# The first microseconds of a gated low-rank kernel: when GpSimd and VectorE subtract, and in which order TensorE takes tile 2

## The reference

```python
base = jnp.einsum('btd,od->bto', x, W)
logits = jnp.einsum('btd,ed->bte', x, Wr)
logits = logits + one_hot(expert_targets, E) * LANG_BIAS          # 5.0
topw, topi = jax.lax.top_k(logits, 2)
weights = jax.nn.softmax(topw, axis=-1)
gates = jnp.sum(one_hot(topi, E) * weights[..., None], axis=-2)
h = jnp.einsum('btd,erd->bter', x, A)                              # E = 8, R = 16
lora_out = jnp.einsum('bter,bte,eor->bto', h, gates, B)
return x + base + 2.0 * lora_out
```

## Time and profile before

| | us |
|---|---|
| median of three runs | 80.66 |
| lowest and highest | 80.62, 80.95 |
| the profiled execution | 80.91 |
| its span, first to last instruction | 79.1 |

### The profile page before, as it was taken

One profiled execution on the slowest core, in us unless ns is written; L12 is line 12 of the kernel. 1 busy time (PEld: TensorE's weight loads), 2 busy tenths in 40 slices (PEclk: granted clock), 3 DMA queues, 4 the chain that ended last, 5 costly groups with the idle time before them and its releaser, 6 DMA issues.

```text
span 79.1 us, 1627 instructions
## 1 busy us (share of the span) xinstructions
PE 75.2 (95%) x505; PEld 71.2 (90%) x505; DVE 49.4 (62%) x219; ACT 22.2 (28%) x56; POOL 24.0 (30%) x26
## 2 busy tenths in 40 slices
PE   6999999799999999999999999999999999999960
PEld 2379997699999999999999999999999999999950
DVE  0099498878692828475483928284664829787670
ACT  4334951514231414050322314140503113111200
POOL 4035697062350241406060503315060605000000
PEclk9999999999999999999999999999999999999999
DMA  1999994489379199998920000270000063032024
GB/s 11 292 321 355 401 420 202 50 364 391 38 273 413 75 227 440 418 298 353 413 109 3 0 0 0 99 298 0 0 0 0 0 264 134 0 133 103 34 102 164
DMA packets 3748, 14.23 MB, mean 180 GB/s; under 512 B 416, under 2 KB 1056, under 8 KB 3488
## 3 DMA queue, kind: packets, MB, share of 16 engines
q1 hardware_dynamic: 3600, 13.98, 48.4%
q10 hardware_dynamic: 144, 0.20, 0.8%
HBM read 9.99 MB, written 4.19 MB: 179 GB/s over the span
## 4 chain that ended last, share of the span: by engine, by line
PE 78%; DMA 8%; DVE 6%; SPq 2%; ACT 1%; issue 1%; DVEq 0%
PE heads_ps L412 36%; PE base_ps L412 25%; DMA first_sb<-in_first 8%; PE heads_ps L444 5%; PE base_ps L444 5%; DVE w_lo L345 3%; PE base_ps L448 2%; PE heads_ps L448 2%; PE ghT_ps L435 2%; SPq L167 1%; ACT w_hi L228 1%; SPq L165 1%; DVE top_atf L297 1%; DVE out_sb L331 1%; ACT x_hi L225 1%
## 5 line engine op out<-in xcount | busy, mean ns | idle before, releaser
L205 POOL TENSOR_TENSOR x_lo<-xT_sb,x_hi 128x512 fp32r<-128x512 f32 x14 | 18.2, 1303 | 37.4 <-ACT x_hi L235 37.4
L412 PE MATMUL heads_ps<-w_hi,x_hi 128*128 128x392 f32 x64 | 22.7, 366 | 0.0
L412 PE MATMUL heads_ps<-w_hi,x_lo 128*128 128x392 f32 x64 | 21.4, 342 | 0.0
L412 PE MATMUL heads_ps<-w_lo,x_hi 128*128 128x392 f32 x64 | 21.1, 339 | 0.0
L412 PE MATMUL base_ps<-w_hi,x_hi 128*128 128x256 f32 x64 | 17.7, 287 | 0.0
L412 PE MATMUL base_ps<-w_hi,x_lo 128*128 128x256 f32 x64 | 17.6, 281 | 0.0
L412 PE MATMUL base_ps<-w_lo,x_hi 128*128 128x256 f32 x64 | 17.5, 282 | 0.0
L281 DVE TENSOR_TENSOR ghT_lo<-ghT_ps,ghT_hi 128x128 fp32r<-128x128 f32 x15 | 4.3, 290 | 15.2 <-ACT ghT_hi L239 15.2
L412 PEld LDWEIGHTS heads_ps<-w_hi,x_hi 128*128 128x128 f32 x64 | 12.0, 192 | 1.1 <-ACT x_hi L225 0.6
L239 ACT ACTIVATE ghT_hi<-ghT_ps 128x128 fp32r<-128x128 f32 x15 | 4.1, 277 | 30.8 <-PE ghT_ps L435 30.8
L412 PEld LDWEIGHTS base_ps<-w_lo,x_hi 128*128 128x128 f32 x64 | 12.1, 189 | 0.3 <-DVE w_lo L345 0.3
(11 more groups left out here) (43 smaller groups left out, 93.4 us busy)
## 6 DMA issues: line engine op xcount, KB each, us to landing
x_sb<-in_x SPq DMA_DIRECT2D x4, 768.0 KB, 5.6
out<-out_sb SPq DMA_DIRECT2D x4, 768.0 KB, 4.2
xT_sb<-in_xT SPq DMA_DIRECT2D x3, 768.0 KB, 4.3
first_sb<-in_first SPq DMA_DIRECT2D x3, 454.0 KB, 5.5
xT_sb<-in_xT SPq DMA_DIRECT2D x1, 1024.0 KB, 6.4
x_sb<-in_x SPq DMA_DIRECT2D x1, 1024.0 KB, 11.1
out<-out_sb SPq DMA_DIRECT2D x3, 256.0 KB, 2.0
xT_sb<-in_xT SPq DMA_DIRECT2D x1, 256.0 KB, 6.4
```

The source lines that it names most:

```text
L205: nc.gpsimd.tensor_tensor(x_lo[:, s, :], xT_sb[:, t - len(FIRST), :], x_hi[:, s, :].bitcast(FP32), ALU.subtract).then_inc(x_lo_made, 1)
L412: return nc.tensor.matmul(dst, xs[:, s, chunks[k]], ws[:, k, cols], start=(k == 0 and n == 0), stop=(k == KC - 1 and n == last_n))
```

## The change

Four things change, all of them before tile 3:

1. VectorE also rounds the heads columns of w_hi in chunk 2, which ScalarE did together with the base columns. TensorE's waits follow that.
2. GpSimd waits until all eight low-weight subtractions are done before x_lo of tile 2.
3. GpSimd waits for gh of tile 0 before b_lo.
4. TensorE takes the heads products of tile 2 in another order: first the eight that need only x_hi, then, one ahead of the transpose of tile 0 and three behind it, those with x_lo.

```diff
+            pool.wait_ge(w_lo_made, 2 * KC)
             x_lower(2, 2)
             pool.wait_ge(b_hi_made, 1)
+            pool.wait_ge(gh_made, 1)
             nc.gpsimd.tensor_tensor(b_lo[:, :], b_sb[:, :], b_hi[:, :].bitcast(FP32),
                                     ALU.subtract).then_inc(b_lo_made, 1)
...
-                w_upper(k, base_cols if k == 1 else all_cols)
+                w_upper(k, base_cols if k < KC - 1 else all_cols)
...
-            dve.wait_ge(chunk_landed[0], 16)
-            heads_upper(1)
-            dve.wait_ge(wh_hi_made, 2)
-            w_lower(1, heads_cols)
-            dve.wait_ge(w_hi_made, 2)
-            w_lower(1, base_cols)
-            for k in range(2, KC):
+            for k in range(1, KC - 1):
+                dve.wait_ge(chunk_landed[k - 1], 16)
+                heads_upper(k)
+                dve.wait_ge(wh_hi_made, k + 1)
+                w_lower(k, heads_cols)
                 dve.wait_ge(w_hi_made, k + 1)
-                w_lower(k, heads_cols)
                 w_lower(k, base_cols)
+            dve.wait_ge(w_hi_made, KC)
+            w_lower(KC - 1, heads_cols)
+            w_lower(KC - 1, base_cols)
...
-                if k == 1:
-                    pe.wait_ge(wh_hi_made, 2)
+                if k < KC - 1:
+                    pe.wait_ge(wh_hi_made, k + 1)
                 else:
-                    pe.wait_ge(w_hi_made, k + 1)
+                    pe.wait_ge(w_hi_made, KC)
                 for t in FIRST:
                     heads_product(t, k, 0)
-                if k == 1:
-                    pe.wait_ge(w_hi_made, 2)
+                pe.wait_ge(w_hi_made, k + 1)
...
-            tile_ready(2)
-            heads(2, (0, 1))
+            pe.wait_ge(x_hi_made, 1)
+            for k in range(KC):
+                for n in range(2):
+                    heads_product(2, k, n)
+            pe.wait_ge(x_lo_made, 1)
+            heads_product(2, 0, 2)
             pe.wait_ge(ident_made, 1)
             transpose(0, 0)
-            heads(2, (2, 3)).then_inc(heads_done, 1)
+            for k in range(1, KC):
+                last = heads_product(2, k, 2)
+            last.then_inc(heads_done, 1)
```

## The result

The changed kernel takes 82.21 us in the median of four runs (82.06 to 82.96), against 80.81 for the kernel before on the same chip. The ratio is 1.0161, with a 95% interval from 1.0117 to 1.0205. It is slower, as forecast, but by 1.3 to 1.4 us where 0.83 was forecast, and outside the range. Its profiled execution took 82.06 us with a span of 80.3.

The account below looks back on a forecast made before the run. TensorE, busy 75.2 of 79.1 us, was taken as the bound. Early gains put it 0.86 us ahead, but held VectorE instructions moved tile 1's transpose from 16.77 to 17.60: 80.66 + 0.83, given as 81.5 us, range 80.5 to 82.0.

Parts of the forecast that it names:

- The tile 0 part of the sum: TensorE up to the first lora product: transpose of tile 0 at 14.17 instead of 14.50, 0.86 us ahead by lora.
- the hold of the cast of tile 1: VectorE's top-index cast (top_atf) starts at 14.75 inside GpSimd's b_lo and ends at 15.45 instead of 14.92, 0.53 us late.
- x_lo of tile 3 on its old distance: GpSimd's x_lo of tile 3 isn't late: it starts 1.66 us after gh of tile 0, at 15.69, ending at 16.98.
- the shift going through to the end: After the transpose of tile 1, distances stay as before, only shifted, so its 0.83 us delay reaches the end.
- 0.07 us ahead of chunk 2: TensorE at 8.89 waits for w_hi of chunk 2; smaller ScalarE piece was to gain 0.07 us.
- 0.25 ahead of the base products of chunk 3: TensorE loses 0.25 us before tile 2 on low base weights of chunk 3; freeing their subtraction was to gain it.
- the cast of tile 0 held for 0.255: VectorE's top_atf of tile 0 takes 0.425 us beside GpSimd's b_lo; free of it, 0.170.
- held the gate: VectorE's gate of tile 1 starts 0.26 behind x_lo of tile 3, ends at 17.01; transpose at 17.60; chance 0.58.
- The prediction's rival: VectorE's `second` of tile 1 is held by x_lo of tile 3: transpose at 17.86, +1.09, 81.8 us; chance 0.14.
- The third cast of heads weights: VectorE's added rounding of w_hi in chunk 2, in an idle stretch; costed at nothing, bounds 0 to 0.1 us.
- The small instructions aren't held: VectorE's small instructions run free beside GpSimd: transpose of tile 1 at 16.24, 0.53 ahead, 80.1 us; chance 0.12.
- The gate gets by: Gate of tile 1 escapes x_lo of tile 3: transpose at 16.77, no change, 80.7 us; chance 0.10.

## Why the prediction was right and wrong

**Direction and most of the mechanism: right.** The tile 0 part of the sum came as written: no idle before the base products of chunk 3, tile 2 from 12.57 (12.45 forecast), the cast of tile 0 at 0.17, gh ending at 14.15 (14.03), the transpose at 14.29 (14.17). So came the hold of the cast of tile 1 (0.73 of some 0.7), x_lo of tile 3 on its old distance (15.82 is 1.67 after gh, 1.66 forecast), TensorE idle for over 1 us, and the shift going through to the end.

**The step that failed most: the kernel before that the gains were counted against.** The forecast took three things off the first profile of before as stable: 0.07 us ahead of chunk 2, 0.25 ahead of the base products of chunk 3, and the cast of tile 0 held for 0.255. They belong to one order of landing, and in the second and third profile of before all three are absent. The one that counts is the hold of the cast: the 0.25 ahead of the base products lay ahead of a wait for gh anyway (0.66 us), so their gain didn't move the transpose of tile 0. With the logits as the origin, the forecast was a way that grows from 4.70 to 17.60 - 12.00 = 5.60, by 0.90, less 0.07 for earlier logits. Measured is a growth from 4.45 to 5.78, by 1.33. A before whose way is shorter by 0.25 accounts for more than half of the 0.43 between the two. This rests on three profiles of before and on the landings of all fourteen; how often its cast is held was not measured directly. The 0.07 of earlier logits goes too: counted from x_hi of chunk 1, the logits start after 6.10 us in the first profile of before, after 6.02 and 5.99 in the others, and after 6.00 and 6.03 in the changed kernel.

**The step that was mis-sized: which instruction meets x_lo of tile 3.** The forecast let `second` pass, with its start 0.05 ahead of x_lo, and held the gate. That so small a lead is enough was my estimate: no row of before has `second` beside a GpSimd subtraction. It was 0.04 ahead and lost, and it lost, 0.03 to 0.04 ahead, in three of three profiles with both b_lo's wait and x_lo in its old place. From the end of gh of tile 0 to the transpose of tile 1 this gives 17.90 - 14.15 = 3.75 instead of the forecast 17.60 - 14.03 = 3.57, 0.18 more. The prediction's rival had 17.86 - 14.03 = 3.83; it took 0.14 us from gh to the transpose of tile 1, where an idle TensorE took 0.06. It had a chance of 0.14, though the earlier trace rows already had an instruction 0.02 ahead losing, and rows of the same trace have gates 0.11 ahead that got through (at 61.69, 0.23 us). The forecast's 0.05 lay between the two, nearer to the one that lost, so the rival deserved more than it got. The experiment with the later x_lo shows the forecast's own case at 3.64, with x_lo 0.15 later than it was.

Together: 0.83 + 0.07 + 0.25 + 0.18 = 1.33, as in the way. It is 1.40 in the medians, 0.07 of which stay open, and 1.15 between the two profiled executions first shown, which had different landings. The before measured beside the result took 80.81 and not the 80.66 that the forecast was added to: 81.49 + 0.57 + 0.15 = 82.21, the measured time. With `second` held alone the prediction stood at 81.8, inside the range.

**Minor.** b_lo began 0.14 after gh of tile 0, the upper of the two bounds. The third cast of heads weights took 0.90 us, not 0.37 like that of chunk 1, since x_lo of chunk 2 had started 0.07 before it (7.83 and 7.89). It was costed at nothing with 0 to 0.1 and did cost nothing visible: TensorE's products run back to back from 8.2 to 12.6.

**The rivals.** "The small instructions aren't held" is refuted by the cast of tile 1, 0.73 to 0.74 us in every profile in which b_lo lies over it. "The gate gets by" came true in part: the gate was free, but only because `second` had already waited out x_lo of tile 3. With that x_lo behind the gates the way is 4.71, level with the 4.70 of the first profile of before, which is where that rival had it; the time is 0.3 above before, as against a way of 4.44.

## What to carry to other kernels

When a GpSimd operation is moved off one short chain on VectorE, look for the next chain that it lands on, and for what the delay of that chain then lines up with. Here a hold of 0.25 us on the cast of tile 0, not even there in every execution, became 0.56 on the cast of tile 1 and another 1.05 on `second`, because a delayed instruction ran into a second GpSimd operation that used to come safely behind it. Count gains that rest on a stall of 0.1 to 0.3 us near the start only if a second profile of the same kernel shows the stall as well. Bulk operations with slack can be put on the engine whose short operations they would hold, in a stretch where it is idle: b_lo took VectorE 0.68 us there and held x_lo of tile 2 for 0.40, which had room, and the way was 4.16, as short as any.

## What the runs showed of the hardware

How small a held instruction can be was known from the earlier trace rows; new is that a 128x8 tensor-scalar operation (`second`) is among them (1.34 for 0.29 us), and how far the starts decide. VectorE instructions that started 0.02 to 0.03 (the late gate of the earlier trace rows, 1.32 to 1.33 us in all fourteen profiles) and 0.03 to 0.04 us (`second`) ahead of the GpSimd one lost. `second` 0.19 ahead, gates 0.11 ahead and a 392-column subtraction 0.09 ahead (6.52 to 6.62 in the changed kernel) won. But it is no plain threshold: low-weight subtractions that follow another one without a gap won from 0.03 ahead (before: 9.28 to 9.30, 0.41 us, while x_lo of chunk 3 took 0.98 for 0.74) and even from 0.02 behind (9.75 to 9.73 in the second profile with the wait for the low weights, 0.41 us, x_lo 1.03). The loss was 1.05 us for `second`, and 0.24 and 0.29 us for x_lo of chunk 3. The order of the starts as a profile shows them does not decide it where they lie within 0.04 us of each other; why one side wins there is not shown. Nor is what fp32r gains: every product with a high or a low part runs in it, 0.178 us for one of 392 columns, and none of them was timed in float32.

The second surprise is the landing of the first chunks: in fourteen profiles the logits of tile 0 began anywhere from 11.85 to 12.99 us (the three of the kernel before: 12.07, 12.12, 12.35; the two of the changed one: 12.12 and 12.53). That spread of 1.14 us is nearly as much as the whole loss. It follows chunk 1, whose rounding on ScalarE starts anywhere from 5.75 to 6.96 us, ahead of all that the edits touch.
